# State steps of a gated delta rule begun inside the first feed-forward pass, and their copies split between two engines

## The chip, the core and the metric

The kernel runs on one core of a Trainium2 chip, in float32 throughout. The metric is the device time of one launch in microseconds (us). A core has TensorE (PE in the profile, with its weight loads as PEld), VectorE (DVE), ScalarE (ACT), GpSimd (POOL) and SyncE (SP), which here only issues DMAs. Each engine works through its own instructions in order and waits on semaphores.

## The reference

The input is x of shape 8 x 1024 x 256. Three blocks follow one another, each with a layer norm in front and a residual behind:

```
x = x + 0.5 * ffn(layernorm(x))
x = x + attn(layernorm(x))
x = x + 0.5 * ffn(layernorm(x))
```

`ffn` is a gated recurrence over the batch axis (8 steps) with a state c for each of 1024 positions, and `attn` is a gated delta rule over the 1024 positions (16 heads of 16, state 16 x 16 for each head and batch):

```
ft, it = sigmoid(xt @ wf.T + c @ uf.T + bf), sigmoid(xt @ wi.T + c @ ui.T + bi)
gt = tanh(xt @ wc.T + c @ uc.T + bc);   c = ft * c + it * gt          # 8 steps, then
h = tanh(x @ wo.T + c_final @ uo.T + bo)

S = S * lam;  err = v_t - k_t S;  S = S + beta * k_t (x) err;  o_t = q_t S     # 1024 steps
```

## The kernel before, in words

The 1024 positions are cut into NB = 8 tiles of 128, and a tile takes 8 FFN steps (one for each batch row, TILE = 8). Everything is written out in a fixed order for each engine.

**First pass** (`first_pe`, `first_act`, `first_dve`, `first_sp`): the first FFN, tile by tile, 64 steps. A step on TensorE is 24 matmuls with x (L420, `ffn_rows`) and 24 with the state (`cst`); ScalarE makes the gates (L436, L443) and VectorE the new state (L458, L462, L464). Beside the steps run **pieces**, the preparation of the attention for the tile before and for the tile before that. Their place is a table, `PERIOD[t]`: at step t of tile b it names pieces of tile b-1 ("prep": `ln2`, `apply`, `lt`, `v01`, `rms`, `v23`, `keys`, `kt`, `km0`, `g01`, `km1`) and of tile b-2 ("solve": `g23`, `gt`, `al`, `inv1` to `inv3`, `tt`, `ta0` to `ta3`). On TensorE the pieces are: `v` (L623), `g` (L648, 128 small matmul records a fill), `lt`/`kt` (L613, L631), `gt` (L763), `tt` (L775) and `ta` (L794, 256 small records each). `ta1` to `ta3` are split in two and laid around a step's halves. Pieces use PSUM banks 4 to 7, handed on by a count of fills and reads (`refill`, `filled`, `emptied`); the FFN steps use banks 0 to 3 by turns.

**Second pass** (`second_pe` and its like): a loop over s of END = 81 turns. In turn s (s < 64) stands **hop** s, which carries the attention's state over 16 positions: `hop_states_pe` (L990, into bank 3), a copy `e` on ScalarE (L1016), `hop_update_pe` (L1007, into banks 4 to 7), and four copies of the new state into `zbd` (L1029 on ScalarE, L1037 on VectorE). For s < 13 ScalarE makes all four copies, later each engine two. SP sends `e` to a tile of rows in SBUF (`hop_sp`, L1057) and loads `xsb` and `kgb` for hop s+2. The first 14 turns hold no FFN step: beside hops 0 to 12 stand the pieces of the last two tiles, by the table `TAIL`, in banks 0 to 2. At s = 14 the second FFN begins (single banks 0 and 1), a step in each turn, in the order states, state half of the step, update, rest of the step, x half of the next step. Once 8 hops of a tile are through, `post_dve`, `post_act` and `post_pool` scale and normalise the attention's rows and add them to x (L1081, L119, L137, L1112 to L1115), about six turns ahead of the tile's second FFN.

```
Y, Z = NB - 2, NB - 1
AT_POST = 8
AT_FFN = AT_POST + 6
END = TILE * NB + AT_FFN + 3
```

## Time and profile before

| | us |
|---|---|
| median of 3 runs | 1770.27 |
| the three runs | 1770.27, 1771.05, 1764.37 |
| the profiled execution, its own time | 1755.78 |
| its span, first to last instruction | 1753.9 |

The profile is of one execution, and its rows are to be set against 1755.78 and 1753.9. A row of a view says engine, source line, operation, the tile written and the tiles read, and a count; "idle" is what its engine waited ahead of it, and for whom. "PEclk" is the granted clock of TensorE as a share of full speed (1.00 is 2.4 GHz, 0.50 is 1.2 GHz).

### The profile page before, as it was taken

Reading aid. Unit: us, or ns where it says so; the run is one execution under the profiler, and the core shown is the slowest. Engines: PE = TensorE matmul, PEld = TensorE weight load, DVE = VectorE, ACT = ScalarE, POOL = GpSimd, SP = SyncE. Lnnn points to the kernel's source line nnn. Section 1 sums busy time; section 2 is a strip of 40 time slices with the busy share of each in tenths; the row PEclk is TensorE's granted clock in tenths of the full one; section 3 lists DMA queues with packets and bytes.
Section 4 is the critical chain, followed back from the end, with each engine's and each line's share of the span. In section 5 each row is a group of like instructions: output and inputs, shape, how many; then the busy total and the mean of one; then the engine's idle time right before and its main releaser. Section 6 shows DMA issues by size and latency. Waiting matters only on the chain.

```text
span 1753.9 us, 61767 instructions
## 1 busy us (share of the span) xinstructions
PE 1427.3 (81%) x27811; PEld 1308.1 (75%) x27811; DVE 875.7 (50%) x2078; ACT 761.6 (43%) x1867; POOL 141.8 (8%) x198
## 2 busy tenths in 40 slices
PE   5898888888878877788665644799999999999977
PEld 5888777777767876677554544798989889898866
DVE  2465747638457475383352161254645455454532
ACT  4464544445335444342242323444445454554432
POOL 0000000000000000000000003040404040412400
PEclk9999988898988998889665555799999999999989
DMA  3011021110110211201322111232333323242100
GB/s 114 1 49 74 27 99 51 57 68 27 75 50 27 99 51 75 68 9 75 103 70 93 57 49 43 86 78 73 103 88 100 99 76 110 67 120 54 53 25 24
DMA packets 55494, 116.96 MB, mean 67 GB/s; under 512 B 10816, under 2 KB 31552, under 8 KB 52160
## 3 DMA queue, kind: packets, MB, share of 16 engines
q1 hardware_dynamic: 55232, 113.03, 20.3%
q8 instruction: 218, 3.57, 0.9%
q14 instruction: 44, 0.36, 0.1%
HBM read 53.74 MB, written 50.86 MB: 60 GB/s over the span
## 4 chain that ended last, share of the span: by engine, by line
PE 62%; DVE 15%; ACT 12%; issue 8%; POOL 1%; SPq 0%; DMA 0%; DVEq 0%; POOLq 0%; ACTq 0%
PE ps L420 30%; PE ps L1007 7%; PE ps L485 5%; PE ps L794 5%; PE ps L990 4%; ACT gates L436 3%; PE ps L623 3%; PE ps L648 3%; DVE ln_bn L119 2%; ACT zbd L1029 2%; ACT gates L443 2%; ACT ffn_rows L137 1%; PE ps L381 1%; DVE inv L703 1%; DVE inv_cols L730 1%
## 5 line engine op out<-in xcount | busy, mean ns | idle before, releaser
L420 PE MATMUL ps<-cst,wt 128*128 128x128 f32 x2688 | 340.8, 281 | 8.8 <-DVE cst L464 8.3
L420 PEld LDWEIGHTS ps<-cst,wt 128*128 128x128 f32 x2688 | 316.6, 194 | 16.1 <-DVE cst L464 8.9
L420 PE MATMUL ps<-ffn_rows,wt 128*128 128x128 f32 x2304 | 309.6, 296 | 16.4 <-ACT ffn_rows L390 5.8
L420 PEld LDWEIGHTS ps<-ffn_rows,wt 128*128 128x128 f32 x2304 | 297.7, 211 | 27.8 <-issue 14.5
L436 ACT ACTIVATE gates<-ps,colv 128x128 f32<-128x128 f32 x448 | 127.2, 366 | 275.0 <-PE ps L420 275.0
L458 DVE TENSOR_TENSOR fc<-gates,cst 128x256 f32<-128x256 f32 x112 | 51.2, 457 | 311.6 <-ACT gates L436 311.2
L1112 POOL TENSOR_TENSOR key_half<-key_half,rowv 128x256 f32<-128x256 f32 x64 | 48.1, 752 | 1518.6 <-ACT key_half L137 1518.6
L1007 PE MATMUL ps<-e,kgb 32*128 32x64 f32 x4032 | 147.0, 301 | 13.6 <-ACT e L1016 13.6
L1007 PEld LDWEIGHTS ps<-e,kgb 32*128 32x128 f32 x4032 | 137.8, 213 | 22.7 <-ACT e L1016 15.8
L794 PE MATMUL ps<-inv_cols,kv 32*32 32x32 f32 x8192 | 89.6, 210 | 58.2 <-issue 49.0
L794 PEld LDWEIGHTS ps<-inv_cols,kv 32*32 32x32 f32 x8192 | 80.4, 112 | 70.1 <-issue 60.6
L1029 ACT COPY zbd<-ps 16x512 f32<-16x512 f32 x152 | 87.6, 576 | 82.1 <-PE ps L1007 79.6
L485 PE MATMUL ps<-wt,ffn_rows 128*128 128x256 f32 x384 | 100.4, 408 | 12.6 <-ACT gates L436 12.5
L1016 ACT COPY e<-ps 128x512 f32<-128x512 f32 x64 | 37.4, 585 | 140.6 <-PE ps L990 140.6
L420 PE MATMUL ps<-kv,wt 128*128 128x128 f32 x768 | 93.0, 277 | 5.9 <-DVE kv L498 3.5
L990 PE MATMUL ps<-zbd,xsb 128*32 128x64 f32 x4096 | 87.0, 243 | 11.4 <-issue 5.9
L648 PE MATMUL ps<-key_half,key_cols 32*32 32x64 f32 x4096 | 57.3, 248 | 47.9 <-issue 25.7
L420 PEld LDWEIGHTS ps<-kv,wt 128*128 128x128 f32 x768 | 88.5, 192 | 9.3 <-issue 5.0
L736 DVE TENSOR_SCALAR xs_out<-ps,w_x 128x512 f32<-128x512 f32 x32 | 37.4, 1170 | 114.6 <-PE ps L794 114.6
L485 PEld LDWEIGHTS ps<-wt,ffn_rows 128*128 128x128 f32 x384 | 74.3, 202 | 25.2 <-ACT gates L436 13.6
L990 PEld LDWEIGHTS ps<-zbd,xsb 128*32 128x32 f32 x4096 | 75.7, 147 | 22.8 <-issue 11.1
L648 PEld LDWEIGHTS ps<-key_half,key_cols 32*32 32x32 f32 x4096 | 48.5, 114 | 53.9 <-issue 49.9
(131 smaller groups left out, 1929.0 us busy)
## 6 DMA issues: line engine op xcount, KB each, us to landing
kg_scratch<-kg_rows SPq DMA_DIRECT2D x8, 2048.0 KB, 7.3
xs_scratch<-xs_out SPq DMA_DIRECT2D x16, 1024.0 KB, 4.3
xsb<-xs_scratch SPq DMA_DIRECT2D x64, 256.0 KB, 3.7
kgb<-kg_scratch SPq DMA_DIRECT2D x256, 64.0 KB, 2.9
ffn_rows<-x SPq DMA_DIRECT2D x8, 1024.0 KB, 5.5
x_scratch<-ffn_rows SPq DMA_DIRECT2D x8, 1024.0 KB, 4.4
ffn_rows<-x_scratch SPq DMA_DIRECT2D x8, 1024.0 KB, 5.8
out<-ffn_rows SPq DMA_DIRECT2D x8, 1024.0 KB, 4.7
```

Of the source, the lines that this page charges most:

```text
L420: mm = pe.matmul(banks[g][:, col:col + P], wt[:, w, k, m * P:(m + 1) * P], rhs, start=(x in (0, FI)), stop=(k == KT - 1 and (t == 0 or x > ...
L436: a = act.activation(gates[q][:, g, m * P:(m + 1) * P], fi[:, g * D + m * P:g * D + (m + 1) * P], ACT.Sigmoid, bias=bias[:, g, m:m + 1])
L458: a = dve.tensor_tensor(fc, gates[q][:, 0, :], cst, ALU.mult)
L485: mm = pe.matmul(self.h_b[j][:, e * D:(e + 1) * D], self.xnT[b.n % len(self.xnT)][:, k, 2 * j + e, :], wt[:, WO, k, :], start=(e == 0 and ...
L623: mm = pe.matmul(dst.ps[:, e * D:(e + 1) * D], xn2T[:, k, 2 * j + e, :], wt[:, WS, k, :], start=(e == 0 and k == 0), stop=(k == KT - 1), s ...
L648: mm[par] = pe.matmul(dst[par].ps[tok, 64 * g:64 * g + 64].rearrange("p (e i) -> p e i", e=2), keyT[row, 8 * gh + g, tok], keyTm[row, :, g ...
L736: dve.tensor_scalar(xs_of(f, 1), src.ps.rearrange("p (k t) -> p k t", t=32), w_x, None, ALU.mult).then_inc(src.read, 1)
L794: mm[par] = pe.matmul(dst[par].ps[32 * c:32 * c + 32, 32 * k:32 * k + 32], kv_of(n)[tok, lane, :], invT[tok, lane, :], start=True, stop=Tr ...
L990: mm = pe.matmul(E_BANK[32 * g:32 * g + 32, 64 * kk:64 * kk + 64], xs_cols[:, k, C * a:C * a + 2 * C], zbd[:, k, :], start=True, stop=True ...
L1007: mm = pe.matmul(S_BANKS[:, k, :], kgb[32 * g:32 * g + 32, a, P * kk:P * kk + P], es[a][32 * g:32 * g + 32, 64 * kk:64 * kk + 64], start=T ...
L1029: act.copy(state_of(zbd, c), state_of(S_BANKS, c)).then_inc(z_done, 1)
L1112: pool.tensor_tensor(yb[:, r, :], yb[:, r, :], rowv[:, 1, :], ALU.mult).then_inc(post_done, 1)
```

## The change

The second pass begins at step JOIN = 48 of one common count i, so the first pass keeps tiles 0 to 5 alone (SOLO = 6). Steps 48 to 63 are the first FFN's tiles 6 and 7, steps 64 to 127 the second FFN. Hop s stands in step i = s + 49, so the first 15 hops lie beside the first FFN's last tiles, and the second FFN begins with no turn between. `TAIL` is gone: the pieces of tiles 6 and 7 keep their places in `PERIOD`, which runs on through the second FFN's tiles 0 and 1, in banks 4 to 7. As hops write the same banks, each piece behind a hop waits for its four state copies (in `refill`), and each hop's update waits until the pieces ahead of it are read. From tile 6 on the FFN has single banks (0 and 1), and `ta` is whole. VectorE makes two of the four state copies from hop 0 on. SP sends `e` to DRAM (`e_scratch`, 4 transfers a hop as before) and once a tile loads the 1 MB of it back into `xn_flat`; `post_*` works there, one turn later than before against the hops. GpSimd's adds of a row vector come one step ahead of its other two operations. `prod` has a buffer of its own, and the wait for the FFN's front ahead of it is gone. The tail of the diff's engine functions for ScalarE and VectorE follows the same order as `second_pe`, which is shown.

```diff
+HOPS = 2 * CHUNKS
+TILE = 8
+SOLO = 6
+JOIN = TILE * SOLO
+FIRST_HOP = JOIN + 1
+SECOND = TILE * NB
+AT_POST = TILE
+END = SECOND + TILE * NB + 3
+
+
+def hop_at(i):
+
+    s = i - FIRST_HOP
+    return s if 0 <= s < HOPS else None
...
     def put(bank, *key):
         table[key] = (bank, counts[bank])
         counts[bank] += 1
+        if bank >= 4:
+            behind_hop[key] = last_hop
...
+    for i in range(JOIN, END):
+        b, t = divmod(i, TILE)
+        n = b - NB
+        if t == 0 and b == NB - 1:
+            singles((4, 5), *four("fr1", b))
+        if t == 0 and n == 0:
+            singles((4, 5), *four("fr2", n))
+        if t == 0 and 0 < n < NB:
             singles((2,), *four("fr2", n, (2, 3)))
-    return table, early, counts
+        if hop_at(i) is not None:
+            last_hop = hop_at(i)
+            ahead_of_hop[last_hop] = list(counts)
+        for behind, name in PERIOD[t] + (PERIOD[TILE] if t == TILE - 1 else []):
+            piece(name, b - behind)
+        if t == TILE - 1:
+            if 0 < n + 1 < NB:
+                singles((2,), *four("fr2", n + 1, (0, 1)))
+            if n < NB:
+                singles((2,), ("ct1", b) if n < 0 else ("ct2", n))
...
+        z_done = sem("p2_z_done")
 
         def refill(pe, *key):
             k, o = FILL[key]
             wait_pos(pe, bank[k].read, o)
+            if BEHIND_HOP.get(key) is not None:
+                pe.wait_ge(z_done, SETS * (BEHIND_HOP[key] + 1))
             return bank[k]
...
-                if n + 2 < NB:
-                    filled(dve, "fr1", n + 2, 3)
-                else:
-                    dve.wait_ge(ff.x_done, 4 * NB)
...
-            if s == 0:
-                for k in range(4, 8):
-                    pe.wait_ge(bank[k].read, EARLY[k])
+            for k in range(4, 8):
+                wait_pos(pe, bank[k].read, AHEAD_OF_HOP[s][k])
...
-            return range(0 if s < len(TAIL) else 2, SETS)
+            return range(2, SETS)
...
-                sp.dma_start(e_of_tile(n)[tok, 4 * P * g:4 * P * (g + 1)],
+                sp.dma_start(e_d[n % 2, tok, 4 * P * g:4 * P * (g + 1)],
...
+            if u == 1:
+                dve.wait_ge(y_in, 16 * (n + 1))
                 dve.wait_ge(alpha_in[b.p], b.landed)
                 for half in range(2):
                     lane = slice(64 * half, 64 * half + 64)
+                    dve.tensor_tensor(by_head(xn_flat)[:, lane, :], by_head(xn_flat)[:, lane, :],
                                       alpha[:, b.p, lane].unsqueeze(2).to_broadcast([P, 64, HD]), ALU.mult).then_inc(y_done, 1)
                 dve.wait_ge(y_done, 2 * (n + 1))
+                ln3.stats_bn(dve, n, xn, bn_buf[1])
+            elif u == 2:
                 ln3.coefficients_bn(dve, n, bn_buf[1])
+            elif u == 5:
                 dve.wait_ge(post_done, POST_OPS * (n + 1))
                 fg.ln.stats_bn(dve, n, xt[b.p], bn_buf[2])
...
             if u == 2:
                 pool.wait_ge(x1_in[p], b.landed)
                 for r in range(8):
+                    pool.tensor_tensor(xt[p][:, r, :], xt[p][:, r, :], rowv[:, 2, :], ALU.add).then_inc(post_done, 1)
+            if u == 3:
+                for r in range(8):
                     pool.wait_ge(ln3.applied, 8 * n + r + 1)
-                    pool.tensor_tensor(yb[:, r, :], yb[:, r, :], rowv[:, 1, :], ALU.mult).then_inc(post_done, 1)
-                    pool.tensor_tensor(xt[p][:, r, :], xt[p][:, r, :], rowv[:, 2, :], ALU.add).then_inc(post_done, 1)
-                    pool.wait_ge(post_done, POST_OPS * n + 3 * r + 2)
-                    pool.tensor_tensor(xt[p][:, r, :], xt[p][:, r, :], yb[:, r, :], ALU.add).then_inc(post_done, 1)
-
-
-        def step_of(s):
-
-            n, t = divmod(s - AT_FFN, TILE)
-            return (Block(n), t) if s >= AT_FFN and n < NB else (None, None)
-
-        def ending(s):
-
-            n, t = divmod(s - AT_FFN, TILE)
-            return Block(n - 1) if t == 0 and 1 <= n <= NB else None
-
-        def starting(s):
-
-            b, u = post_of(s)
-            return b if u == 5 else None
+                    pool.tensor_tensor(xn[:, r, :], xn[:, r, :], rowv[:, 1, :], ALU.mult).then_inc(post_done, 1)
+                    pool.wait_ge(post_done, POST_OPS * n + 8 + 2 * r + 1)
+                    pool.tensor_tensor(xt[p][:, r, :], xt[p][:, r, :], xn[:, r, :], ALU.add).then_inc(post_done, 1)
...
         def second_pe(pe):
+            for i in range(JOIN, END):
+                f, b, t = step_of(i)
+                s = hop_at(i)
+                old, done = ending(i)
+                nxt = starting(i)
+                if s is not None:
                     hop_states_pe(pe, s)
+                for r in range(2):
+                    if t == 0 and f is fg and b.n > 0:
+                        fg.pe_front(pe, b, (2 + r,))
+                    if done is not None:
+                        old.pe_h(pe, done, 2 + r)
+                if i == SECOND or (t == 0 and f is ff and i > JOIN):
+                    f.pe_front(pe, b, range(4))
+                if i == SECOND:
+                    pe.wait_ge(ff.h_read, 5 * NB)
+                if f is not None:
+                    f.pe_step(pe, b, t, *((0, NX) if t == 0 else (NX, NX + FI)))
+                if s is not None:
+                    hop_update_pe(pe, s)
+                if f is not None and t > 0:
+                    f.pe_step(pe, b, t, NX + FI, 2 * NX)
+                if f is not None and t < 7:
+                    f.pe_step(pe, b, t + 1, 0, NX)
+                pieces(pe, *period_of(i), prep_pe, solve_pe)
+                if t == 7 and f is not None:
+                    prep = b.ahead(-1) if f is ff else Block(NB - 1) if b.n == 0 else None
                     for r in range(2):
+                        f.pe_h(pe, b, r)
+                        if prep is not None:
+                            gram_pe(pe, prep.n, r)
+                        if nxt is not None:
+                            fg.pe_front(pe, nxt, (r,))
+                    f.pe_cterm(pe, b)
 
...
         def second_sp(sp):
+            for s in range(2):
+                load_xs(sp, s)
+                load_kg(sp, s)
+            for i in range(JOIN, END):
+                b, t = divmod(i, TILE)
+                s = hop_at(i)
+                cur, u = post_of(i)
+                if u == 0:
+                    n = cur.n
+                    for a in range(2):
+                        sp.wait_ge(aligned[a], 16 * Q * Q * (n + 1))
+                    if n == 0:
+                        filled(sp, "fr1", NB - 1, 3)
+                    else:
+                        filled(sp, "fr2", n - 1, 3)
+                    sp.dma_start(xn_flat, e_d[n % 2]).then_inc(y_in, 16)
                     wait_pos(sp, y_done, 2 * (n - 1))
                     sp.wait_ge(alpha_out, 16 * (n + 1))
                     sp.dma_start(alpha[:, n % 2, :], alpha_d[n]).then_inc(alpha_in[n % 2], 16)
+                if s is not None:
                     hop_sp(sp, s)
+                    if s + 2 < HOPS:
+                        load_xs(sp, s + 2)
+                        load_kg(sp, s + 2)
+                prep, solve = Block(b - 1), Block(b - 2)
+                if t == 0:
+                    if Block(b - 3).real and b > SOLO:
+                        store_xs(sp, Block(b - 3), 1)
+                    if prep.real:
+                        store_x1(sp, prep)
+                if t == 1 and prep.real:
+                    sp.wait_ge(ln2.applied, 8 * (prep.n + 1))
+                    sp.wait_ge(x_out[prep.p], prep.landed)
+                    if prep.ahead(2).real:
+                        sp.dma_start(xt[prep.p], x_v[prep.n + 2]).then_inc(x_in[prep.p], 16)
+                    else:
+                        sp.dma_start(xt[prep.p], x1_d[prep.n + 2 - NB]).then_inc(x1_in[prep.p], 16)
+                if t == 2 and solve.real:
+                    store_alpha(sp, solve)
+                if t == 5 and prep.real:
+                    store_kg(sp, prep)
+                if t == 6 and solve.real:
+                    store_xs(sp, solve, 0)
+                n = b - 1 - NB
+                if t == 1 and n >= 0:
+                    sp.wait_ge(fg.x_done, 4 * (n + 1))
+                    sp.dma_start(out_v[n], xt[n % 2]).then_inc(o_out[n % 2], 16)
+                if t == 2 and n >= 0 and n + 2 < NB:
+                    sp.wait_ge(o_out[n % 2], Block(n).landed)
+                    sp.dma_start(xt[n % 2], x1_d[n + 2]).then_inc(x1_in[n % 2], 16)
```

## Rows read from the trace of the kernel before

**Rows 1.** The page: busy time of each engine, and the span in 40 slices.

```profile
PE 1427.3 (81%) x27811; PEld 1308.1 (75%) x27811; DVE 875.7 (50%) x2078; ACT 761.6 (43%) x1867; POOL 141.8 (8%) x198
...
PEclk9999988898988998889665555799999999999989
```

**Rows 2.** Busy time by stretch: start:end, length, engines (count), clock, DMA.

```profile
34.80:96.00 61.20, 53.57 (x418) 51.40 (x418) 34.46 (x126) 27.98 (x96) 0.00 (x0) 0.94 0.00 1
...
618.60:735.70 117.10, 92.78 (x2040) 84.28 (x2037) 67.62 (x146) 53.33 (x136) 0.00 (x0) 0.90 0.15 57
...
853.70:1121.60 267.90, 154.78 (x4814) 131.59 (x4814) 97.56 (x210) 86.16 (x139) 16.82 (x24) 0.54 0.22 69
1296.70:1378.80 82.10, 78.38 (x1439) 72.99 (x1438) 41.73 (x109) 40.09 (x97) 17.69 (x24) 1.00 0.33 94
1625.20:1695.40 70.20, 57.49 (x467) 52.80 (x466) 31.76 (x93) 26.05 (x74) 18.07 (x24) 0.90 0.10 33
1695.40:1753.90 58.50, 46.70 (x366) 43.73 (x364) 17.24 (x35) 15.63 (x49) 0.00 (x0) 0.96 0.11 36
```

**Rows 3.** Timeline of VectorE: new FFN state after step 0 of tile 7.

```profile
735.67 0.42 DVE L464 TENSOR_TENSOR cst<-fc,ig 128x256 f32<-128x256 f32 x1
```

**Rows 4.** Timeline of one step of second FFN with its hop: start, length.

```profile
1422.27 0.91 POOL L1112 TENSOR_TENSOR key_half<-key_half,rowv 128x256 f32<-128x256 f32 x1
1422.63 0.83 DVE L464 TENSOR_TENSOR cst<-fc,ig 128x256 f32<-128x256 f32 x1
...
1423.45 1.18 PE L990 MATMUL ps<-zbd,xsb 128*32 128x64 f32 x64
...
1424.56 2.05 PE L420 MATMUL ps<-cst,wt 128*128 128x128 f32 x16
1424.70 0.58 ACT L1016 COPY e<-ps 128x512 f32<-128x512 f32 x1 [3.06 <-PE ps L990]
...
1425.31 3.20 SPq L1057 DMA_DIRECT2D kg_rows<-e  x4
...
1426.54 2.01 PE L1007 MATMUL ps<-e,kgb 32*128 32x64 f32 x64
...
1428.62 1.39 DVE L1037 COPY zbd<-ps 16x512 f32<-16x512 f32 x2 [0.38 <-PE ps L1007]
1429.23 1.76 SPq L975 DMA_DIRECT2D kgb<-kg_scratch  x4
...
1430.94 0.43 DVE L464 TENSOR_TENSOR cst<-fc,ig 128x256 f32<-128x256 f32 x1
```

**Rows 5.** Groups by line in tile 6 of first FFN: busy, mean ns, idle.

```profile
L794 PE MATMUL ps<-inv_cols,kv 32*32 32x32 f32 x1024 | 10.6, 200 | 5.2 <-issue 4.2 <-DVE xs_out L736 1.1
...
L648 PE MATMUL ps<-key_half,key_cols 32*32 32x64 f32 x507 | 7.2, 224 | 7.8 <-issue 5.8 <-DVE key_rows L601 2.0
...
L93 ACT ACTIVATE ffn_rows<-ffn_rows,ln_stats 128x256 f32<-128x256 f32 x8 | 4.0, 496 | 0.0
...
L775 PE MATMUL ps<-ident,inv 128*128 128x128 f32 x16 | 2.9, 322 | 5.4 <-DVE inv_cols L730 3.6 <-ACT inv_cols L747 1.9
...
L763 PE MATMUL ps<-ident,key_rows 128*128 128x128 f32 x16 | 2.5, 288 | 2.0 <-DVE inv L703 2.0
...
L583 DVE TENSOR_TENSOR key_rows<-key_rows,rms 128x2048 f32<-128x2048 f32 x1 | 2.3, 2293 | 0.0
```

**Rows 6.** Timeline: the longest gap of TensorE in a run of small matmuls.

```profile
745.73 0.47 PE L648 MATMUL ps<-key_half,key_cols 32*32 32x64 f32 x17 [6.12 <-issue]
```

**Rows 7.** The page: the queue that carries instructions.

```profile
q8 instruction: 218, 3.57, 0.9%
```

**Rows 8.** DMA issues, KB each, us from issue to landing.

```profile
kgb<-kg_scratch SPq DMA_DIRECT2D x256, 64.0 KB, 2.9
...
ffn_rows<-x_scratch SPq DMA_DIRECT2D x8, 1024.0 KB, 5.8
```

**Rows 9.** Timeline near the end: statistics that wait for GpSimd's adds.

```profile
1666.17 2.71 DVE L119 BATCH_NORM_STATS2 ln_bn<-ffn_rows 128x6 f32<-128x256 f32 x8 [0.62 <-POOL ffn_rows L1115]
```

370 lines of the change are left out of this document (147 added, 223 removed).

## The prediction

> **What bounds the kernel now.** I read the page first: TensorE is busy for 81% of the span, ScalarE and VectorE for half or less [rows 1]. That is a mean over stages, so the next view is busy time by stretch [rows 2]. Its bounds are the starts of L464 after step 0 of a tile, such as 735.67 [rows 3]; so a stretch is one tile of 8 steps. Four kinds are to be seen. A tile of FFN steps alone takes 61.2 us, one with the full set of pieces 117.1, one of second-FFN steps with hops 82.1. Between the passes lies a stretch of 267.9 us, 14 turns of hops and pieces with no FFN step, in which TensorE is busy for 154.8 and its granted clock is 0.54, so mostly 1.2 GHz. In the tile of 82.1 the clock is 1.00 and TensorE is busy for 78.4: there it is the bound. The timeline of one such step [rows 4] shows why: states 1.18, state half of the step 2.05, update 2.01, then the rest, each behind the other, while `e` (0.58) and the copies into `zbd` (1.39) lie beside matmuls. In the hop-only stretch nothing stands in those places, and a turn takes 267.9 / 14 = 19.1 us. TensorE is bound by order and waits there, by work elsewhere.
>
> **The change, part by part.** The sum goes along the tiles, counted 0 to 15 over both FFNs, against the span of 1753.9.
>
> *Removed:* the stretch between the passes, 267.9 us. Its hops and pieces come back inside tiles 6 to 9.
>
> *Tiles 0 to 5* keep their order; step 0 of tile 6 ends at 618.6 [rows 2] as now. `prod` of its own takes a wait from VectorE that I cost at nothing: the front that it waited for is long done.
>
> *Pieces* cost 117.1 - 61.2 = 55.9 us a tile beside FFN steps. *Hops with FFN steps and the work behind them* make a tile of 82.1. As TensorE's order is what is full in both, I add: 82.1 + 55.9 = 138.0 for tiles 7 and 8. Tile 6 has seven hops: less (82.1 - 61.2) / 8 = 2.6, so 135.4. Tile 9 has only the solve half of the pieces. By busy and idle time that is `ta` 15.8, `tt` 8.3, `gt` 4.5 and half of `g` 7.5, together 36.1 [rows 5]; I take 33, as these rows hold low clock, so 115.1. For comparison, TensorE's busy time would be 78.4 + 92.8 - 53.6 = 117.6 of the 138.0, still the bound.
>
> *Tiles 10 to 13:* 4 x 82.1 = 328.4. *Tile 14* has only the last hop: 70.2 now, 58.3 to 70.2 possible. GpSimd's adds end late there and the statistics wait for them [rows 9]; with eight of the 24 moved ahead, 8 x 0.75 = 6 us go (24 take 18.07 [rows 2]): 64. Its bounds go into the range. *Tile 15 to the end:* 58.5 [rows 2].
>
> Sum so far: 618.6 + 135.4 + 138.0 + 138.0 + 115.1 + 328.4 + 64 + 58.5 = 1596.0.
>
> *New waits.* (a) A piece's bank waits for the four state copies, and two of these now stand in VectorE's queue, behind that step's pieces. The worst is `keys`, three operations of 2.3 us [rows 5]: the copies at step 5 come some 7 us late, the FFN state with them. TensorE meanwhile has the rest of the step, 4 us, and then stalls for the remainder. I lay the steps of one tile end to end and find 0 to 3 us at steps 4, 5 and 7, more where the attention's normalisation joins (tiles 7 and 8). (b) The update waits until the pieces ahead are read; states and the state half, 3.2 us [rows 4], lie between and cover a short evacuation. If several queue up, it shows. (c) ScalarE's layer-norm sums at steps 3 and 4 of tile 6 stand ahead of `e`; their squares alone take 4.0 a tile [rows 5] and the state half covers 2.05: 3 us. (d) `ta` is whole, so 256 small records come in a row, then 64 of the states. TensorE already stops in such runs with nothing to wait for, 6.12 us at the longest [rows 6], 5.8 and 4.2 us a tile in sum [rows 5]. The instruction queue brought 218 packets of 16.4 KB [rows 7] for 2 x 27811 records of TensorE, so one packet holds about 255 of them: I read the stops as late instructions and take 1 us a tile. The Trainium skill (Runtime: NRT & Kernel Launch, Instruction fetch mechanics) gives the same block of 256 instructions, and calls the crossing of a block mostly hidden; by that the 1 us a tile would be nought. The trace's gap of 6.12 us speaks against it. Together (a) to (d): 5, 7, 7 and 3 us for tiles 6 to 9, 22. Their floor is 0, if all fits in present idle time. Their ceiling is that every hop shows its whole chain, 1.18 + 0.58 + 2.01 + 1.39 = 5.2 in place of TensorE's 3.2 [rows 4], 31 x 2.0 = 62 us. I stay near the low end, since in rows 4 the copies do hide.
>
> *GpSimd against VectorE.* While GpSimd adds, the same VectorE operation takes 0.83 instead of 0.43 [rows 4]. GpSimd's 24 operations a tile now run beside `inv3`, `rms` and `keys`. At 0.4 each that is 9.6 us a tile at most, and never below 0; I take half in tiles 7 and 8 and 3.5 in tile 9: 13.
>
> *Clock.* The tile with pieces has 0.90 [rows 2], some 23 us at half rate. With the hops in it TensorE's gaps fill, and I take back 3 us in each of tiles 6 to 8: -9. Bounds: 0 and -6 each.
>
> *SP's queue.* A step's issues take 3.20 for `e` and 1.76 for `kgb` of the 8.3 us between two L464 [rows 4]. The pieces' stores and the reload of `e` now stand between. The reload (5.8 us to landing by the row of the same size [rows 8]) has a turn until VectorE needs it, and hop loads are two turns ahead at 2.9 us to landing: nothing, as long as turns last 14 us or more. If that cover fails, see the fourth case.
>
> *State copies.* In 13 hops ScalarE makes all four; two take VectorE 1.39 [rows 4], so at best one such spell goes from each chain. Beside 4 us of matmuls that hides, and the price is in (a).
>
> Sum: 1596.0 + 22 + 13 - 9 = **1622.0** span. The profiled run lies 1.9 above its span: 1623.9. The median of the runs shown is 1770.27 / 1755.78 = 1.008 times the profiled run, so I forecast a median of **1637**.
>
> **The rivals.**
> 1. *Forecast*, 1610 to 1665: tiles 6 to 9 at 120 to 150 us.
> 2. *TensorE alone sets the pace.* New waits and the GpSimd term are nought: 1622 - 35 = 1587 span, 1602 as a median; with tile 14 at 58.3 it is 1596. For: VectorE is busy for 67.6 of 117.1 [rows 2]. Against: in just that tile TensorE idles a fifth, so VectorE's order does count.
> 3. *VectorE's queue sets the pace.* Every hop shows its chain, 62 in place of 22: 1662 span, 1677 as a median. The like would come from a stricter rule on the port: if each of GpSimd's 24 operations held VectorE for its whole 0.73 us, three tiles would give 52 in place of 13, 1661 and 1677 again. The Trainium skill (SBUF — State Buffer, SBUF: two separate sides) says this: a lock held for the whole instruction, the loser fully blocked. By that rule the price is 0.73. The trace shows a wait, but one of 0.4 on average. Both together give 1716.
> 4. *Slower: SP's queue.* It issues in order, and store of x, reload and waits for `ff.x_done` and `ln2.applied` stand ahead of `kgb` for hop s+2. If the load of each hop came a turn late, update s would wait for issue and landing and the transfers of `e` ahead, 3.2 + 1.8 + 2.9 = 7.9 us, 31 times: 1622 + 245 = 1867 span, 1884. It decides from (1753.9 - 1622) / 31 = 4.3 us a hop. For: the issues already fill 5.0 of 8.3 us. Against: turns become 15 us and more.
> 5. *Nothing overlaps:* the cross waits between pieces and hops serialise so that each of the 14 turns removed comes back at 19 us; 1770. Against: rows 4 show a hop and a step overlapping under the same semaphores.
>
> **How the numbers follow.** Chances: forecast 0.60, TensorE alone 0.14, VectorE's queue 0.17, slower 0.05, nothing overlaps 0.04. The range takes in cases 1 and 2 down to 1590, and case 3 up to 1700: about 0.86 with the parts of case 3 above it left out. A measurement of this kernel can tell about 0.5%, 9 us, from no change. Cases 1 to 3 are all faster by more than that, 0.91; case 5 is within it, 0.04; case 4 is slower, 0.05.
>
> **What would show it.** Right: no stretch at clock 0.5 between the passes; the first L990 near 625 us; L464 after step 0 comes about 137, 147, 147 and 122 us after the one before it for tiles 7, 8, 9 and 10, then every 82; the mean clock of tiles 6 to 9 above 0.90; the state copies on VectorE in all hops, with their wait for L1007 short. Wrong: TensorE waiting for `zbd` of VectorE for over 2 us a hop (case 3); `kgb` landings ending waits of L1007 (case 4); clock 0.5 staying in tiles 7 to 9.

## The result and the profile after

The changed kernel takes **1748.56 us** as the median of 4 runs (1735.13 to 1754.53), against 1767.85 for the kernel before (4 runs): a ratio of 0.9881 with a 95% interval of 0.9846 to 0.9916. It is 1.2% faster; 7.5% was forecast (1637), and the range ended at 1700. The profiled execution is the slowest of the four, 1754.53 us with a span of 1752.7.

The page first: busy time by engine, the granted clock in 40 slices and the instruction queue. They answer to [rows 1] and [rows 7].

```profile
PE 1439.7 (82%) x27811; PEld 1319.9 (75%) x27811; DVE 907.6 (52%) x2104; ACT 745.7 (43%) x1841; POOL 161.5 (9%) x198
...
PEclk9999988898889988788878888787799999999999
...
q8 instruction: 219, 3.59, 0.9%
```

The stretch at clock 0.5 between the passes is gone, as forecast. What came in its place is a long band of 7 and 8. The view by stretch says where it lies; the bounds are again the starts of the cell update (now L493) after step 0, so the rows are tiles 6 to 10, 14 and 15, and the columns are those of [rows 2].

```profile
627.60:787.20 159.60, 133.07 (x3083) 120.27 (x3082) 79.02 (x162) 67.64 (x160) 0.00 (x0) 0.84 0.21 68
787.20:962.90 175.70, 129.55 (x3072) 116.25 (x3072) 96.78 (x209) 64.83 (x136) 25.43 (x24) 0.83 0.23 75
962.90:1138.70 175.80, 132.50 (x3071) 118.17 (x3070) 95.30 (x205) 63.52 (x133) 25.66 (x24) 0.81 0.23 74
1138.70:1287.40 148.70, 112.90 (x2752) 103.98 (x2751) 69.98 (x155) 50.94 (x111) 18.70 (x24) 0.82 0.25 75
1287.40:1373.70 86.30, 80.44 (x1439) 74.41 (x1438) 42.72 (x109) 40.21 (x98) 17.94 (x24) 0.98 0.37 112
...
1622.90:1694.20 71.30, 58.41 (x414) 53.90 (x413) 32.16 (x93) 25.46 (x74) 19.30 (x24) 0.90 0.09 30
1694.20:1752.70 58.50, 46.71 (x366) 43.74 (x364) 17.24 (x35) 15.63 (x50) 0.00 (x0) 0.96 0.11 37
```

Against the terms of the sum, whose new waits, GpSimd and clock are laid on tiles 6 to 9 as the prediction did:

| stretch | forecast us | measured us | difference |
|---|---|---|---|
| to the start of tile 6 | 618.6 | 627.6 | +9.0 |
| tile 6 | 137.4 | 159.6 | +22.2 |
| tile 7 | 146.8 | 175.7 | +28.9 |
| tile 8 | 146.8 | 175.8 | +29.0 |
| tile 9 | 121.6 | 148.7 | +27.1 |
| tiles 10 to 13 | 328.4 | 335.5 | +7.1 |
| tile 14 | 64 | 71.3 | +7.3 |
| tile 15 | 58.5 | 58.5 | 0 |

Tiles 6 to 9 took 659.8 us for 553 forecast, 107 us more, and that is the miss. Before, the same work took 678.1 (both tiles with pieces, the stretch between the passes and the rest up to the same point of tile 10), so of 125 us that were to be won 18 were. Put per turn: the 14 turns removed came back at (659.8 - 410.2) / 14 = 17.8 us each, where they had cost 19.1. The first row is no loss: the code up to there is the same, and over this profile and those of the experiments it took 617.1 to 635.1.

Two columns of tile 7 split its 28.9 us. By the prediction's own rows TensorE should have been busy for 117.6 - 3 = 114.6 and idle for 32.2. It was busy for 129.6 and idle for 46.1: 15 us more of the one and 14 of the other. In tile 6 it is busy time alone (133.1, idle 26.5). The instruction counts are as expected, so the same matmuls took longer. The view by line of tile 6, TensorE alone (last figure ahead of the second bar: mean ns of one):

```profile
L448 PE MATMUL ps<-cst,wt 128*128 128x128 f32 x168 | 29.0, 337 | 0.0
...
L1010 PE MATMUL ps<-e,kgb 32*128 32x64 f32 x512 | 18.1, 294 | 3.6 <-ACT e L1019 3.5
L994 PE MATMUL ps<-zbd,xsb 128*32 128x64 f32 x512 | 13.4, 269 | 3.6 <-issue 3.6
```

The same view of the kernel before, for a tile of second-FFN steps with hops (1296.7 to 1378.8):

```profile
L420 PE MATMUL ps<-cst,wt 128*128 128x128 f32 x168 | 22.5, 284 | 0.0
...
L1007 PE MATMUL ps<-e,kgb 32*128 32x64 f32 x512 | 16.1, 273 | 0.0
L990 PE MATMUL ps<-zbd,xsb 128*32 128x64 f32 x512 | 9.4, 225 | 0.0
```

Three groups with the same counts took 60.5 us in place of 48.0. That is the clock: sorted by the granted clock at their start, the records of tile 6 that began at full clock have the mean durations of the kernel before to within 1 ns (284, 274 and 226 ns for the three groups, in the order of its rows), and those that began at half clock 432, 416 and 312 ns. (512 updates also say that the stretch holds eight hops and not the seven that I subtracted for: 2.6 us.) How it is lost is to be seen in three windows of tile 7, TensorE only, whose columns are its busy time, its clock and the DMA's:

```profile
842.00:848.00 6.00, 6.00 (x153) 1.00 0.25 64
848.30:854.60 6.30, 0.00 (x0) 0.65 0.16 42
854.70:860.10 5.40, 5.40 (x25) 0.50 0.00 0
```

Full clock, a gap of 6.3 us in which it falls, then the half of the FFN step at 1.2 GHz. The timeline has these 24 matmuls, here behind the gap and then in the kernel before at full clock (start, duration):

```profile
854.66 5.49 PE L448 MATMUL ps<-ffn_rows,wt 128*128 128x128 f32 x24 [6.42 <-ACT gates L465]
```

```profile
1502.83 2.84 PE L420 MATMUL ps<-ffn_rows,wt 128*128 128x128 f32 x24
```

They take 5.49 us in place of 2.84. Every fall to 1.2 GHz in tile 7 stands in or right behind an idle time of TensorE of 1.4 to 7 us. By the records of the clock the half rate lasts 51, 61, 68 and 55 us in tiles 6 to 9, 236 together; it was 24 in tile 6 before.

What ends these gaps is the next view, the waits of TensorE in tile 7 (us in total, times, longest):

```profile
PE ps L815 <- issue: 12.7, 4, 5.6
PE ps L815 <- DVE zbd L1040: 6.8, 1, 6.8
PE ps L448 <- ACT gates L465: 6.4, 1, 6.4
PE ps L994 <- issue: 4.7, 2, 2.7
...
PE ps L649 <- DVE zbd L1040: 3.1, 1, 3.1
```

The largest names no engine at all, and the two of over 6 us have one cause, which the names hide. The timeline around the second (start, duration, engine, line):

```profile
917.65 2.71 DVE L119 BATCH_NORM_STATS2 ln_bn<-ffn_rows 128x6 f32<-128x256 f32 x8
...
923.27 0.17 DVE L131 SCALAR_TENSOR_TENSOR ln_stats<-ln_bn,ln_stats 128x8 f32<-128x8 f32 x1
923.48 2.07 ACT L137 ACTIVATE ffn_rows<-ffn_rows,ln_stats 128x256 f32<-128x256 f32 x4 [6.14 <-DVE ln_stats L131]
925.46 1.10 ACT L465 ACTIVATE gates<-ps,colv 128x128 f32<-128x128 f32 x4
...
926.93 1.39 DVE L1040 COPY zbd<-ps 16x512 f32<-16x512 f32 x2
...
928.47 1.55 PE L815 MATMUL ps<-inv_cols,kv 32*32 32x32 f32 x131 [6.78 <-DVE zbd L1040]
```

ScalarE had nothing to do for 6.14 us, because the next instruction in its queue was the normalisation of the post part (L137), whose coefficients VectorE was still computing. Behind it stood the gates of the FFN step, though their bank had been ready since 918.7 (`cst` half of the step, 2.05 us from 916.61). Behind the gates stood VectorE's cell update and copies, and behind these TensorE. The same row with 7.66 us stands at 851.52, and the gap of 6.3 us above lies in that wait. In tiles 10 to 13, where VectorE has no pieces, the longest wait of L137 in a tile is 3.0 us and the clock stays at 0.98 or more.

### The profile page after: what moved, and what is told of

Its sections match the earlier page's. It is cut to its first block, busy times and chain, and to the rows that moved or that the text cites. A ratio compares the mean times of both kernels' runs of the same rounds, so it can differ in the third digit from the quotient of the medians.

```text
span 1752.7 us, 61952 instructions
## 1 busy us (share of the span) xinstructions
PE 1439.7 (82%) x27811; PEld 1319.9 (75%) x27811; DVE 907.6 (52%) x2104; ACT 745.7 (43%) x1841; POOL 161.5 (9%) x198
## 4 chain that ended last, share of the span: by engine, by line
PE 58%; DVE 18%; ACT 11%; issue 10%; DMA 0%; SPq 0%; DVEq 0%; ACTq 0%
PE ps L448 29%; PE ps L515 7%; PE ps L1010 5%; PE ps L815 5%; PE ps L994 3%; ACT gates L465 3%; PE ps L674 3%; PE ps L649 3%; DVE ln_bn L119 2%; ACT ffn_rows L137 2%; DVE prod L743 2%; DVE inv L746 1%; ACT gates L472 1%; PE ps L408 1%; DVE ig L491 1%
## 5 line engine op out<-in xcount | busy, mean ns | idle before, releaser
L448 PE MATMUL ps<-cst,wt 128*128 128x128 f32 x2688 | 366.3, 293 | 10.9 <-DVE cst L493 9.0
L448 PEld LDWEIGHTS ps<-cst,wt 128*128 128x128 f32 x2688 | 337.9, 204 | 21.8 <-DVE cst L493 10.1
L465 ACT ACTIVATE gates<-ps,colv 128x128 f32<-128x128 f32 x448 | 127.1, 365 | 247.4 <-PE ps L448 247.4
L1099 POOL TENSOR_TENSOR ffn_rows<-ffn_rows,rowv 128x256 f32<-128x256 f32 x64 | 54.9, 892 | 1372.9 <-DMA ffn_rows<-x_scratch 1372.9
L1010 PE MATMUL ps<-e,kgb 32*128 32x64 f32 x4032 | 129.9, 276 | 7.9 <-ACT e L1019 6.9
L1010 PEld LDWEIGHTS ps<-e,kgb 32*128 32x128 f32 x4032 | 121.2, 190 | 16.5 <-issue 10.5
L137 ACT ACTIVATE ffn_rows<-ffn_rows,ln_stats 128x256 f32<-128x256 f32 x192 | 99.1, 593 | 71.0 <-DVE ln_stats L131 68.5
L515 PE MATMUL ps<-wt,ffn_rows 128*128 128x256 f32 x384 | 106.8, 428 | 9.5 <-ACT gates L465 8.9
L994 PE MATMUL ps<-zbd,xsb 128*32 128x64 f32 x4096 | 91.2, 248 | 20.3 <-issue 15.7
L994 PEld LDWEIGHTS ps<-zbd,xsb 128*32 128x32 f32 x4096 | 79.1, 148 | 32.9 <-issue 23.6
L1040 DVE COPY zbd<-ps 16x512 f32<-16x512 f32 x126 | 85.8, 681 | 25.8 <-PE ps L1010 23.1
L1032 ACT COPY zbd<-ps 16x512 f32<-16x512 f32 x126 | 72.7, 577 | 54.6 <-PE ps L1010 52.8
L774 ACT ACTIVATE xs_out<-ps,w_x 128x512 f32<-128x512 f32 x32 | 39.1, 1222 | 129.1 <-PE ps L815 123.1
```

The source lines that it names most:

```text
L137: act.activation(dst[:, b, :], src[:, b, :], ACT.Identity, bias=self.nm[:, b:b + 1], scale=self.rs[:, b:b + 1]).then_inc(self.applied, 1)
L448: mm = pe.matmul(banks[g][:, col:col + P], wt[:, w, k, m * P:(m + 1) * P], rhs, start=(x in (0, FI)), stop=(k == KT - 1 and (t == 0 or x > ...
L465: a = act.activation(gates[q][:, g, m * P:(m + 1) * P], fi[:, g * D + m * P:g * D + (m + 1) * P], ACT.Sigmoid, bias=bias[:, g, m:m + 1])
L515: mm = pe.matmul(h_b[j][:, e * D:(e + 1) * D], self.xnT[b.n % len(self.xnT)][:, k, 2 * j + e, :], wt[:, WO, k, :], start=(e == 0 and k == ...
L994: mm = pe.matmul(E_BANK[32 * g:32 * g + 32, 64 * kk:64 * kk + 64], xs_cols[:, k, C * a:C * a + 2 * C], zbd[:, k, :], start=True, stop=True ...
L1010: mm = pe.matmul(S_BANKS[:, k, :], kgb[32 * g:32 * g + 32, a, P * kk:P * kk + P], es[a][32 * g:32 * g + 32, 64 * kk:64 * kk + 64], start=T ...
```

## The experiments

The theories on record were mainly these: the half clock costs most of it (C); instructions that come late (I); VectorE's order (V) and ScalarE's (H, head of the line); GpSimd against VectorE (P). Each run is compared with the kernel before on its own chip, so the ratios are comparable, and to 0.9881 of the change. The second measure is the length of tiles 6 to 9 in the run's profile, with TensorE's time at half clock and its gaps there, the stretches of over 0.3 us without a record of a matmul or of a weight load: 659.8, 236 and 144 us for the change.

The second measure is one profile each, and a coarse one: tiles 0 to 5, whose code no run touches, took 617.1 to 635.1 us, and the change's profile is of an execution 6 us above its median. A difference in the tiles of under 10 us is therefore not clear of noise, and neither is a difference of two ratios of under 0.005 or so, 9 us, as each has an interval of 0.003 to 0.004 to either side. Where the two measures part, I say so.

**All four state copies on ScalarE in the first 31 hops** (the change without its second half)

```diff
         def by_act(s):
-            return range(2, SETS)
+            return range(0 if s < 31 else 2, SETS)
```

> Edit: ScalarE makes all four state copies for hops 0 to 30, those that stand beside pieces; VectorE none of them. Theory V (VectorE's queue holds TensorE up: its copies stand behind normalisation and pieces, and the next piece's bank waits for them): the gaps of TensorE that end on VectorE's zbd copy, about 3.1 and 6.8 us in tile 7, go, and the stretch of tiles 6 to 9 falls from 659.8 us by 25 to 40. Theory I (TensorE stops for late instructions in runs of small matmuls): at most 10 us less, as the gaps marked issue stay. If ScalarE's longer chain (2.3 us for 1.4) counts: up to 31 x 0.9 = 28 us more.

Measured: 1753.53 us (10 runs), ratio 0.9949 (0.9923 to 0.9975); tiles 6 to 9 659.8, half clock 212, gaps 147. The waits in tile 7:

```profile
PE ps L815 <- ACT zbd L1032: 7.3, 1, 7.3
PE ps L448 <- ACT gates L465: 7.2, 1, 7.2
```

The gap of 6.8 us is still there and has only changed the name of its releaser. So it was not VectorE's copy, and theory V alone is refuted. By the profiles the edit gives nothing in these tiles, but this profile is of the fastest of the ten executions, 10 us below their median. By the times it costs 0.7%, 12 us (the two intervals do not meet, by 0.0007), which fits the third expectation, ScalarE's longer chain; so the sharing of the copies, the second half of the change, seems to have earned something after all.

**`ta` cut in two, with a half of an FFN step between**

```diff
+                cut = t in (5, 6, 7) and i // TILE - 2 < NB
...
+                if cut:
+                    solve_pe(pe, i // TILE - 2, f"ta{t - 4}", (0,))
+                    if t < 7:
+                        f.pe_step(pe, b, t + 1, NX // 2, NX)
+                    else:
+                        f.pe_h(pe, b, 0)
+                    solve_pe(pe, i // TILE - 2, f"ta{t - 4}", (1,))
```

> Edit: in the second loop ta1, ta2 and ta3 are again cut in two halves on TensorE, as in the first pass, with half of the next step's x matmuls (or an output matmul group) between. Theory I: idle time marked issue ahead of ta, 20.4 us in tile 7 on the weight-load side, falls by a half or more, and tiles 6 to 9 get 20 to 35 us shorter; fewer stretches at half clock. Theory V: within 5 us of the changed kernel, since VectorE's waits are untouched, or slightly longer as the first half now waits for the copies 1 us earlier.

Measured: 1746.34 us, ratio 0.9899 (0.9869 to 0.9928); tiles 6 to 9 654.0, half clock 218, gaps 138. A gain of 5.8 us in the tiles and none that the times can show. The stops of `ta` marked issue fall from 41.7 to 24.9 us over the four tiles, but of the 20 to 35 us that theory I promised for them next to nothing arrives.

**The store of `kg_rows` (2048 KB each by the page) issued five steps later, at step 2 of the next tile**

```diff
-                if t == 5 and prep.real:
-                    store_kg(sp, prep)
+                    if b > SOLO:
+                        store_kg(sp, solve)
```

> Edit: the store of kg_rows (2 MB, 7.6 us to landing) is issued at step 2 of the next tile and not at step 5, where it lies beside ta1. Theory I in its strict form (bulk transfers hold back the instruction packets): the 5.6 us gap in ta1 falls to about 2, 3 to 4 us a tile, 10 to 15 us over tiles 6 to 9. If the burst alone drains the instructions and the transfer is a bystander: no change within 4 us. Theory V: no change.

Measured: 1738.93 us, ratio 0.9858 (0.9831 to 0.9886); tiles 6 to 9 653.0, half clock 229, gaps 138. The timeline of the change around the store, and then that of this run at the same place:

```profile
886.07 0.42 SPq L841 DMA_DIRECT2D kg_scratch<-kg_rows  x1
...
887.23 2.17 PE L815 MATMUL ps<-inv_cols,kv 32*32 32x32 f32 x227
895.02 0.46 PE L815 MATMUL ps<-inv_cols,kv 32*32 32x32 f32 x29 [5.62 <-issue]
```

```profile
877.90 2.10 PE L815 MATMUL ps<-inv_cols,kv 32*32 32x32 f32 x227
882.21 0.46 PE L815 MATMUL ps<-inv_cols,kv 32*32 32x32 f32 x29 [2.21 <-issue]
```

Both runs stop behind the same record, the 227th, with nothing to wait for that the profile shows; only the length differs, 5.62 us with the store under way and 2.21 without it. In the change each stop of TensorE in this tile that is marked issue ends 1.3 to 1.6 us after a packet of the instruction queue has landed (all nine of over 0.3 us), and for this one the packet landed at 893.6. The stop is a late block of instructions. That a bulk transfer makes it later rests on more than this pair: in the five other profiles that leave the store and `ta` as they are, this stop in tile 7 lasts 5.2 to 6.0 us, and the second one of tile 9, where no store stands, at most 2.3. The gain of 6.8 us in the tiles is less than the 10 to 15 expected and not clear of noise.

**GpSimd's operations cut to 4 of 256 columns in the first three tiles**

```diff
+            w = 4 if n < 3 else D
...
-                    pool.tensor_tensor(xn[:, r, :], xn[:, r, :], rowv[:, 1, :], ALU.mult).then_inc(post_done, 1)
+                    pool.tensor_tensor(xn[:, r, 0:w], xn[:, r, 0:w], rowv[:, 1, 0:w], ALU.mult).then_inc(post_done, 1)
```

> Edit: GpSimd's scale and adds of the first three tiles work on 4 of 256 columns, so this leaves out most of the affine part and the residual there; all semaphores stay. Theory P (GpSimd against VectorE on a shared path): VectorE's inv and prod operations at step 2 fall from 1.03 to 0.6 us and keys from 2.8 to 2.3; tiles 7 to 9 get 10 to 20 us shorter. Theories V and I: VectorE's order only matters where TensorE waits for it, 5 us or less.

Measured: 1741.39 us, ratio 0.9865 (0.983 to 0.9901); tiles 6 to 9 646.1, half clock 215, gaps 138. VectorE by line and form in tile 7, the change and then this run:

```profile
L607 DVE TENSOR_TENSOR kg_rows<-key_rows,hs 128x2048 f32<-128x2048 f32 x1 | 2.8, 2829 | 0.0
...
L743 DVE TENSOR_TENSOR prod<-inv 128x448 f32<-128x448 f32 x2 | 2.1, 1033 | 0.1
```

```profile
L607 DVE TENSOR_TENSOR kg_rows<-key_rows,hs 128x2048 f32<-128x2048 f32 x1 | 2.3, 2302 | 0.0
...
L743 DVE TENSOR_TENSOR prod<-inv 128x448 f32<-128x448 f32 x2 | 1.3, 636 | 0.1
```

An operation of VectorE that reads two tiles is 0.4 to 0.5 us longer while GpSimd works, whether it takes 0.64 or 2.3 alone, and so it is a wait for one operation of GpSimd and not a slower rate. The timeline of the change shows that GpSimd waits in turn, and for longer:

```profile
877.38 2.83 DVE L607 TENSOR_TENSOR kg_rows<-key_rows,hs 128x2048 f32<-128x2048 f32 x1
878.14 2.65 POOL L1105 TENSOR_TENSOR ffn_rows<-ffn_rows 128x256 f32<-128x256 f32 x1
...
880.76 2.77 POOL L1103 TENSOR_TENSOR ffn_rows<-ffn_rows,rowv 128x256 f32<-128x256 f32 x1
```

GpSimd's 0.72 us become 2.65, and they end 0.58 us after VectorE's operation has ended. The two take turns, a whole operation each. In the tiles 13.7 us come back, as expected, but by the times 3 us, so what the path costs this kernel stays open between 0 and 13.

**The post part's normalisation put behind the step's gates and copies on ScalarE**

```diff
-                post_act(act, i, 0)
+                if i >= SECOND + 2 * TILE:
+                    post_act(act, i, 0)
...
+                if i < SECOND + 2 * TILE:
+                    post_act(act, i, 0)
                 post_act(act, i, 1)
```

> Edit: up to step 80 the first half of ScalarE's normalisation (ln3 and the second FFN's norm, L137) stands behind the step's gates, state copies and pieces, and not ahead of the gates. Theory H (head of line: the normalisation on ScalarE waits for VectorE's coefficients, the gates wait behind it, and TensorE's next x matmuls and ta wait for the gates' bank): the gaps of 6.4 and 6.7 us in tile 7 go or fall below 2, and so in tiles 8 and 9; with the half clock behind each, tiles 6 to 9 get 25 to 45 us shorter than 659.8. Theory I (late instructions) and V (VectorE's own chain is that late anyway): 8 us or less.

Measured: 1733.33 us, ratio 0.9829 (0.9791 to 0.9867); tiles 6 to 9 645.4, half clock 236, gaps 126. Waits of TensorE in tile 7:

```profile
PE ps L815 <- issue: 12.7, 4, 6.0
...
PE ps L796 <- DVE zbd L1040: 4.0, 1, 4.0
PE ps L815 <- DVE zbd L1040: 3.2, 1, 3.2
```

The wait for the gates is out of the list, and so are all six waits of L137 for VectorE in tiles 7 to 9, which were 2.7 to 7.7 us. The tiles are 14.4 us shorter, where 25 to 45 were expected; by the times it is 9 us, and the two intervals still meet. What stands there now is the next in line, VectorE's copies: 4.0 and 3.2 us. The stops without a releaser are untouched.

**TensorE's gaps filled with matmuls that nobody reads**

```diff
+                pe.matmul(ps[2], wt[:, WF, 0, 0:P], wt[:, WI, :, :].rearrange("p k m -> p (k m)"), start=True, stop=True,
+                          skip_group_check=True)
...
+                    if part == 1:
+                        fill_time(pe, 2)
...
+                if t == 3 and i >= TILE * 7:
+                    fill_time(pe, 2)
+                if t == 4:
+                    fill_time(pe, 3)
+                if t == 7 and i >= TILE * 7:
+                    fill_time(pe, 4)
```

> Edit: matmuls of weights into PSUM bank 2 that nobody reads, 128x512 each, at the places where TensorE stood idle in tiles 6 to 9: two inside each ta, two ahead of v01, three ahead of tt, four ahead of ta3. They compute nothing and add 40 to 50 us of TensorE work. Theory C (the half clock that follows each gap is the large term): time at half clock in tiles 6 to 9 falls from 236 us to under 80 and these tiles get 20 to 60 us shorter in spite of the added work. If the clock is a by-stander, they get 10 to 40 us longer. Without an effect on the clock: longer by what does not fit the gaps.

Measured: 1753.41 us (9 runs), ratio 0.9942 (0.9913 to 0.997); tiles 6 to 9 659.8, half clock 140, gaps 108. The filler in tile 7 (durations: least, median, longest):

```profile
L789 PE MATMUL ps<-wt x34: 592/592/1061, 828.8 to 929.7; 128*128 128x512 f32 x34
```

The half clock falls by 96 us, so it does follow from the gaps. The theory's own forecast missed: under 80 us at half clock and 20 to 60 us shorter tiles. In tiles 6 to 9 the filler takes 65.3 us, gaps shrink by 36, and all other work of TensorE takes 491.0 in place of 513.9 (time with a record of its matmuls or weight loads): 22.9 us for 96, or **0.24 us lost per us at half clock**. A second way gives nearly the same. In the change's own trace, the time from one record's start to the next is 225 ns at half clock and 121 at full for the state half of the step, 27 and 15 ns for the states, 10 and 9 for `ta`, whose median is 7 at both; such differences summed over all groups of tiles 6 to 9 give some 62 us for 236, or 0.26. That price is the useful result; by the profiles the filler spends what it earns, and by the times it costs 0.6%, 11 us, with intervals that just meet.

**VectorE's part of post cut in the first three tiles** (the scaling of `y` and the two statistics)

```diff
-                    lane = slice(64 * half, 64 * half + 64)
+                    lane = slice(64 * half, 64 * half + (4 if n < 3 else 64))
...
-                ln3.stats_bn(dve, n, xn, bn_buf[1])
+                ln3.stats_bn(dve, n, xn, bn_buf[1], 16 if n < 3 else D)
...
-                fg.ln.stats_bn(dve, n, xt[b.p], bn_buf[2])
+                fg.ln.stats_bn(dve, n, xt[b.p], bn_buf[2], 16 if n < 3 else D)
```

> Edit: VectorE's scaling and both sets of statistics of the attention's first three tiles work on a sixteenth of the columns, which leaves out most of that work; the coefficients (some 3 us twice) and all semaphores stay. About 7 us of VectorE time go in each of tiles 7 to 9. Theories V and H: the gaps ahead of v01, tt and ta3 shrink by 2 to 3 us each and the tiles get 15 to 30 us shorter together. Theory I: below 8 us.

Measured: 1731.21 us, ratio 0.9812 (0.9771 to 0.9854); tiles 6 to 9 642.6, half clock 212, gaps 136. The tiles are 17.2 us shorter, 12 us by the times, of the size of the reordering above, at which the work stays whole. That it comes from earlier coefficients is only in part seen: ahead of L137 ScalarE's second wait in tile 7 falls from 6.1 to 3.7 us, but the first is 8.5 after 7.7.

**The three edits that keep the work together: late normalisation, later store, `ta` cut**

```diff
+                if i < SECOND + 2 * TILE:
+                    post_act(act, i, 0)
...
+                        store_kg(sp, solve)
...
+                    solve_pe(pe, i // TILE - 2, f"ta{t - 4}", (0,))
```

> Edit: three together: ScalarE's normalisation behind the gates up to step 80, the 2 MB store of kg_rows at step 2 of the next tile, ta1 to ta3 cut in two on TensorE. If the causes are separate their gains add: tiles 6 to 9 at 659.8 less 25 to 45 (H) less 5 to 10 (store) less 3 to 8 (split), a median of 1690 to 1720. If one wait only takes the place of another: within 10 us of the best of the three alone.

Measured: 1723.51 us, ratio 0.9773 (0.9737 to 0.9808); tiles 6 to 9 630.2, half clock 198, gaps 115. In the tiles the three alone sum to 14.4 + 6.8 + 5.8 = 27.0 us and together give 29.6, as separate causes would. By the times they sum to 9 + 4 - 3 = 10 us and together give 19. With the noise of both measures this does not show that they add; it does show that the three together beat the change, and the median is just outside the 1690 to 1720 expected.

**The same, with all four copies on ScalarE**

```diff
         def by_act(s):
-            return range(2, SETS)
+            return range(0 if s < 31 else 2, SETS)
```

> Edit: the three of e8 and, with them, all four state copies on ScalarE for hops 0 to 30. Theory H+V (two waits lie one behind the other: once the gates no longer wait behind ScalarE's normalisation, TensorE waits for VectorE's zbd copies, which stand behind the same coefficients, 3.1, 4.0 and 3.2 us in tile 7 of e5): these go too, 15 to 30 us less than e8's 630.2 in tiles 6 to 9, a median of 1695 to 1710 where e8 had 1723.5. Theory H alone (the copies were never worth anything, as e1 by itself showed): within 8 us of e8, or up to 10 us slower by ScalarE's longer chain.

Measured: 1705.65 us (6 runs), ratio 0.966 (0.9627 to 0.9692); tiles 6 to 9 618.1, half clock 177, gaps 103. The waits in tile 7:

```profile
PE ps L815 <- issue: 5.1, 3, 2.3
...
PE ps L815 <- ACT zbd L1032: 1.8, 3, 1.5
```

The edit that gave 0 in the tiles by itself, and cost 12 us by the times, gives 12.1 us in the tiles here and 20 by the times (0.9773 to 0.966, intervals apart), and no wait for `zbd` above 1.5 us is left in tile 7.

**Half of `ta`'s matmuls left out in tiles 6 to 9**

```diff
-                    for k in range(8 * part, 8 * part + 8):
+                    for k in range(8 * part, 8 * part + (4 if n > 3 else 8)):
```

> Edit, on the changed kernel: each ta of tiles 6 to 9 does 64 of its 128 small matmuls, so half of the solved rows of four tiles is left out. TensorE's own time for the part left out is 5.5 us a tile (11.0 of L815 in tile 7), 22 us over four. Theory I (runs of small matmuls end in waits for instructions, and the half clock follows): with the shorter runs the stops of 12.7 us a tile mostly go, so tiles 6 to 9 get 50 to 75 us shorter and time at half clock falls by 60 us or more. Rivals (V, H): 20 to 30 us shorter, the matmuls' own time and little else.

Measured: 1688.15 us, ratio 0.9569 (0.9523 to 0.9615); tiles 6 to 9 603.1, half clock 181, gaps 115. The first waits in tile 7:

```profile
PE ps L448 <- ACT gates L465: 7.9, 1, 7.9
PE ps L815 <- DVE zbd L1040: 6.8, 1, 6.8
```

The stops of `ta`, 12.7 us in this tile and 41.7 in the four, are gone in all four; those behind the normalisation stand as they were, and one of 2.8 us marked issue is new ahead of L1010. Own time left out is 4 x 5.5 = 22 us (half of 11.0 us a tile), the tiles are 56.7 shorter. Of the other 35 us, 29 are gaps and some 6 are less busy time; the half clock fell by 55 us, which by the price above would be 13. The times say the same, 0.9881 to 0.9569, 55 us. This is what theory I foretold, 50 to 75 us, and 20 to 30 by its rivals.

**The best version so far with a light filler**

```diff
+                if t == 4:
+                    fill_time(pe, 2)
...
+                    if t == 4 and name == "ta0":
+                        fill_time(pe, 1)
...
+                    if part == 1:
+                        fill_time(pe, 1)
```

> Edit: e9 and one matmul of 128x512 that nobody reads between the halves of each ta, two ahead of tt and one ahead of ta0, in tiles 6 to 9, some 28 in all and 25 to 30 us of TensorE work. Theory C: time at half clock falls by a third or more and pays for the work, so the median lies within 10 us of e9's, on either side. If the gaps that are left are long ones elsewhere, the clock stays as it is and the median is 15 to 25 us above e9's.

Measured: 1699.12 us, ratio 0.9633 (0.9602 to 0.9664); tiles 6 to 9 613.0, half clock 116, gaps 87. The median is the lowest of the kernels that do all the work, but its interval overlaps that of the version without filler, so a gain is not shown. The half clock did fall by a third, from 177 us, and TensorE's other work by 11.8 us: 0.19 us for each us at half clock, beside the 0.24 above.

**Late normalisation (its edit is above) and four copies on ScalarE, nothing else**

```diff
         def by_act(s):
-            return range(2, SETS)
+            return range(0 if s < 31 else 2, SETS)
```

> Edit, on the changed kernel: ScalarE's normalisation behind the gates up to step 80 (as e5) and all four state copies on ScalarE for hops 0 to 30 (as e1), and nothing else. Theory H+V (two waits one behind the other): e5 alone had 645.4 us in tiles 6 to 9 and e1 alone 659.8, as the changed kernel; together they give 630 to 637, a median of 1712 to 1724, and no wait of TensorE in tile 7 that ends on zbd. If the gain of e9 over e8 came from something else (the store or the split beside the copies): within 5 us of e5's 645.4 and a median near 1733.

Measured: 1717.89 us (6 runs), ratio 0.973 (0.9695 to 0.9765); tiles 6 to 9 626.9, half clock 201, gaps 110. Two waits in tile 7 show what is left:

```profile
PE ps L815 <- issue: 11.7, 4, 5.2
...
PE ps L815 <- ACT zbd L1032: 1.5, 1, 1.5
```

Against the late normalisation alone the tiles win 18.5 us, and the ratio falls from 0.9829 to 0.973, 17 us, with the intervals apart. Against the change itself the two edits give 32.9 us in the tiles and 27 by the times. Here both measures agree on the sign and nearly on the size: four copies on ScalarE cost 12 us with the normalisation ahead of the gates and win 17 with it behind. So the two edits depend on each other: as long as the normalisation stands ahead, ScalarE's copies are late with everything else on ScalarE. Over tiles 6 to 9 TensorE waited 15.4 us for the gates L465 and 27.3 for VectorE's `zbd` in the change, none and 22.9 with the normalisation moved alone, and with both edits 6.0 for `zbd`, now ScalarE's.

## Why the prediction was wrong

**What held.** The stretch of 267.9 us is gone, and its work stands in tiles 6 to 9 with the counts that the sum along TensorE assumed, but for one hop in tile 6. Tile 7 has 3072 TensorE records; one with pieces and one with hops, less the plain FFN, come to 2040 + 1439 - 418 = 3061. Tiles 10 to 13 took 83 to 86 us each, tile 15 took 58.5. The SP queue (case 4) never became a bound: no wait for `kgb` appears among those of tile 7. GpSimd against VectorE was put at 13 us for three tiles, and taking it away gave 13.7 in the tiles, but 3 by the times, so the term is not refuted and not confirmed. Case 3's 52 us, the whole 0.73 for each of GpSimd's operations, came in neither measure. The Trainium skill (SBUF — State Buffer, SBUF: two separate sides) has the loser blocked for the whole instruction, and the trace agrees: GpSimd's 0.72 us became 2.65 behind an operation of VectorE. What case 3 had wrong is the price drawn from it: by these rows the loser waits for what is left of one operation, 0.4 to 0.5 us on VectorE's side, and only where the two meet.

**Step that failed first: the clock.** "With the hops in it TensorE's gaps fill, and I take back 3 us in each of tiles 6 to 8: -9." They did not fill: tile 6 has 24 us of gaps of over 0.3 us (23 before), tile 7 has 45. Added matmuls lie between the gaps and not in them, for a gap is a wait in the order of the engines. So the falls of the clock stayed, and more work stood behind each. The mean clock of tiles 6 to 9 was to be above 0.90 and is 0.81 to 0.84. The 3 us taken back imply, at the filler's price, about 12 us a tile left at half clock (with tile 9 counted alike, 48); 236 in the four tiles were measured, and (236 - 48) x 0.24 makes 45 us of the 107, as an estimate. I had taken a high mean of busy time for a filled engine.

**Step that failed second: the new waits, 22 us.** Point (a) looked for late copies in VectorE's queue. The order that blocked was ScalarE's: I listed the layer-norm sums ahead of `e` under (c), but not the post part's normalisation, which in the stretch between the passes had been harmless since nothing of an FFN stood behind it. It waits for coefficients of VectorE, and the gates stand behind it: 6.4 and 6.8 us in tile 7, and with it moved 14.4 us less over the tiles (9 by the times). VectorE's copies, my (a), come out only when that is gone, and then cost 12 to 20 us by the two measures. Together the waits for the gates and for `zbd` are 42.7 us in the four tiles, where (a) to (d) had 22 for everything. I had asked what is queued behind a waiting instruction for VectorE alone.

**Third: late instructions, (d), 1 us a tile.** The stops ahead of the weight loads of `ta` in one tile (waits of the weight-load queue: us in total, times, longest) were, in tile 6 before:

```profile
PEld ps L794 <- issue: 6.0, 5, 2.4
```

and in tile 7 after:

```profile
PEld ps L815 <- issue: 20.4, 6, 6.9
```

The mechanism was right and its size was not: 14 us more in tile 7 on the weight-load side, and on the matmul side, which the sum counts, 12.7 for 4.2 [rows 5], 8.5 us more where I had 1. The half of `ta` that was left out freed 35 us beyond its own time. I counted only the longer run of small matmuls, and left out that a store under way makes a packet later (5.62 against 2.21 us). That the 128 records which a hop adds a turn have a part in it is likely, but no run tested it by itself. The Trainium skill (Runtime: NRT & Kernel Launch, Instruction fetch mechanics) gives the block of 256, which agrees with 219 packets for 2 x 27811 records; "mostly hidden" does not agree here, with 12.7 us of stops in one tile's `ta`.

**Tile 14.** It took 71.3 us for 64 forecast and 70.2 before, though it no longer holds even the last hop (no record of L994 in it, 64 of L990 before), which the prediction had wrong too. Of the 6 us for eight adds moved ahead nothing came. GpSimd did end earlier, but the statistics that waited for it [rows 9] start at nearly the same place:

```profile
1665.33 0.42 DVE L493 TENSOR_TENSOR cst<-fc,ig 128x256 f32<-128x256 f32 x1
1665.67 2.70 DVE L119 BATCH_NORM_STATS2 ln_bn<-ffn_rows 128x6 f32<-128x256 f32 x8
```

They stand behind this step's cell update in VectorE's queue, 42.8 us into the tile, and before they stood 41 us into theirs. GpSimd had set them back by 0.62 us [rows 9] and not by 6.

**The rivals.** The result lies between case 3 (1677, or 1716 with both its halves) and case 5 (1770), nearer to case 5, which had a chance of 0.04: 17.8 us of its 19 came back for each turn. Its reason, cross waits between pieces and hops, is a part of it (the waits for `zbd`), beside the clock and the late instructions that it did not name. Case 3 had the kind right, an engine's order that sets the pace, and the engine wrong. No case joined several waits with the clock that each of them takes down, and such a case would have come near: +14 us of idle and +15 of slow matmuls in tile 7. The ceiling of 62 us on waits was worked out from one hop's chain, and a blocked queue is not bounded by that.

**What stays open.** The best version without filler still has 618.1 us where 553 was forecast, with 177 us at half clock and 103 of gaps. By the price above some 30 of the 65 us are the clock; the rest was not taken apart further. Whether a shorter code of `ta` (fewer, larger matmuls) would end the stops was not tried.

## What to carry to other kernels

When two phases are merged, go through every in-order queue, ScalarE's as well, and ask of each instruction that waits for another engine what of the *other* phase now stands behind it; a wait that was free in its own phase stalls the merged one, and putting it behind the step's gates was the cheapest gain here (9 to 14 us of 660, 27 to 33 together with the copies that it had masked). Don't expect added work to raise TensorE's clock unless it lands in the very gaps, and price each gap with the slow matmuls behind it. An edit that gives nothing alone, or costs 12 us, can be worth 12 to 20 us once the wait in front of it is gone, so repeat such tests after each repair. And set the profile of one execution beside the median of its kernel's runs before reading a gain from it.
